# Keys and values from one pair of combined matrices in a fused two-layer block on one NeuronCore

## What is computed

```python
q = x @ Wq
k = x @ Wk
v = x @ Wv
latent_kv = (k + v) @ W_down_kv
k_rec = latent_kv @ W_up_k
v_rec = latent_kv @ W_up_v
...
qh, kh, vh = (heads(q), heads(k_rec), heads(v_rec))
...
scores = jnp.einsum('bhqd,bhkd->bhqk', qh, kh) * scale
...
decay = jnp.exp(-LAMBDA_DECAY * TIME_STEP * jnp.abs(idx[:, None] - idx[None, :]))
scores = scores * decay[None, None, :, :]
...
attn = jax.nn.softmax(scores, axis=-1)
```

## Time and profile before

| | |
|---|---|
| median of 3 runs | 816.33 us (816.19 to 817.85) |
| profiled execution, its own time | 818.78 us |
| its span, first to last instruction | 817.0 us |
| mean granted TensorE clock | 0.919 |
| TensorE busy | 703.0 us (86%) |
| ScalarE busy | 574.4 us (70%) |
| VectorE busy | 496.3 us (61%) |
| GpSimd busy | 261.1 us (32%) |

### The profile page before, as it was taken

One profiled execution on the slowest core, in us unless ns is written; L12 is line 12 of the kernel. 1 busy time (PEld: TensorE's weight loads), 2 busy tenths in 40 slices (PEclk: granted clock), 3 DMA queues, 4 the chain that ended last, 5 costly groups with the idle time before them and its releaser, 6 DMA issues.

```text
span 817.0 us, 11157 instructions
## 1 busy us (share of the span) xinstructions
PE 703.0 (86%) x3624; PEld 410.8 (50%) x3624; DVE 496.3 (61%) x1268; ACT 574.4 (70%) x807; POOL 261.1 (32%) x289
## 2 busy tenths in 40 slices
PE   2789889899898998999686697999999999999587
PEld 2566566576566676778454342223323232233364
DVE  4799879788787988889565542234323232222474
ACT  4657675656777666656444436999999999999243
POOL 3376466665666564556403000021200000000020
PEclk9999999999999999999657776999999999999958
DMA  9002322222233333333100269100079300000001
GB/s 260 3 0 67 91 91 91 78 93 76 80 95 88 91 104 103 95 116 104 51 1 0 58 138 195 23 1 1 1 144 193 79 1 1 1 1 1 3 1 51
DMA packets 31342, 54.53 MB, mean 67 GB/s; under 512 B 4625, under 2 KB 13281, under 8 KB 29777
## 3 DMA queue, kind: packets, MB, share of 16 engines
q1 hardware_dynamic: 30128, 53.38, 25.1%
q0 software_dynamic: 224, 0.34, 0.2%
q10 hardware_dynamic: 928, 0.06, 0.1%
HBM read 35.71 MB, written 1.28 MB: 45 GB/s over the span
## 4 chain that ended last, share of the span: by engine, by line
ACT 28%; PE 17%; issue 7%; DVE 6%; POOL 2%; ACTq 0%; POOLq 0%; DVEq 0%
ACT raw_w L827 25%; PE bank L1391 3%; PE bank L1392 2%; PE bank L1393 2%; PE bank L1680 1%; ACT xt L644 1%; POOL act_parts L574 1%; PE bank L1431 1%; PE bank L1515 1%; PE bank L1512 1%; PE bank L1587 1%; PE bank L1513 1%; PE bank L1446 1%; PE bank L1664 1%; DVE xn_parts L920 1%
## 5 line engine op out<-in xcount | busy, mean ns | idle before, releaser
L827 ACT ACTIVATE raw_w<-bank,minus_c 128x1024 f32<-128x1024 f32 x256 | 259.6, 1165 | 4.8 <-DVE bank L1271 2.6
L574 POOL TENSOR_TENSOR act_parts<-act,act_parts 128x512 fp32r<-128x512 f32 x128 | 167.7, 1312 | 147.4 <-ACT act_parts L716 142.0
L1271 DVE TENSOR_TENSOR bank<-bank,fix 128x256 f32<-128x256 f32 x128 | 55.3, 433 | 180.7 <-PE bank L1664 180.7
L702 ACT ACTIVATE bank<-bank,b_gate 128x512 f32<-128x512 f32 x112 | 74.1, 661 | 86.1 <-PE bank L1393 85.9
L1391 PE MATMUL bank<-xn_parts,w_hi 128*128 128x512 f32 x256 | 110.4, 431 | 20.9 <-DVE up L1044 11.5
L1393 PE MATMUL bank<-xn_parts,w_hi 128*128 128x512 f32 x256 | 104.3, 407 | 0.0
L1392 PE MATMUL bank<-xn_parts,w_lo 128*128 128x512 f32 x256 | 104.0, 406 | 0.0
L716 ACT ACTIVATE act_parts<-act 128x512 fp32r<-128x512 f32 x128 | 80.3, 628 | 23.4 <-DVE act L1062 21.9
L1044 DVE TENSOR_SCALAR up<-bank,b_up 128x512 f32<-128x512 f32 x113 | 84.0, 744 | 20.5 <-PE bank L1393 19.3
L1062 DVE SCALAR_TENSOR_TENSOR act<-up,bank 128x512 f32<-128x512 f32 x128 | 87.9, 687 | 4.4
L520 POOL TENSOR_SCALAR var_eps<-mean_var 128x4 f32<-128x4 f32 x28 | 7.2, 256 | 237.8 <-DVE mean_var L914 236.4
(11 more groups left out here) (198 smaller groups left out, 1089.2 us busy)
## 6 DMA issues: line engine op xcount, KB each, us to landing
grow<-scores SPq DMA_DIRECT2D x68, 256.0 KB, 3.2
early<-scores SPq DMA_DIRECT2D x44, 256.0 KB, 3.1
raw_w<-in_gate_up SPq DMA_DIRECT2D x4, 512.0 KB, 8.7
w_lo<-gelu_parts SPq DMA_DIRECT2D x8, 256.0 KB, 5.1
w_lo<-act_parts SPq DMA_DIRECT2D x8, 256.0 KB, 5.2
w_hi<-gelu_parts SPq DMA_DIRECT2D x6, 256.0 KB, 4.6
w_hi<-act_parts SPq DMA_DIRECT2D x6, 256.0 KB, 5.5
x_tok<-in_x SPq DMA_DIRECT2D x4, 256.0 KB, 4.4
```

Source lines behind the costliest of these rows:

```text
L574: pool.tensor_tensor(act_lo[:, j % NACT, :], act[:, j % NACT, :], act_hi[:, j % NACT, :].bitcast(F32), ALU.subtract).then_inc(s["lo_ready" ...
L702: eng.activation(out, bank[:, G, :], ACT.Gelu_apprx_sigmoid, bias=b_gate[:, e:e + 1]).then_inc(s["glu_ready"], 1)
L827: eng.activation(probs[:, u % NP, :], pair, ACT.Exp, bias=minus_c[:, b:b + 1])\
```

## The change

(Wk + Wv) W_down_kv W_up is worked out once, beside the expert loop. GpSimd adds Wk and Wv (slot 13). TensorE transposes the sum (slot 106), multiplies it with w_down (slot 109) and that with both w_up side by side (slot 112), in the bank `SIDE`; ScalarE copies each result out (slots 107, 110, 113) and the last one is split into `sq_hi` and `sq_lo`, the lo part by VectorE (slot 114), in place of Wk and Wv. Keys are then three passes from the norm, like queries, and values are three passes for each block of 128 tokens, straight from the norm. `keys_values` and `latents` and their copies are gone.

The low parts of queries and keys of chunks 0 and 1 move from VectorE to GpSimd. The copy of keys of chunks 2 and 3 moves from VectorE to ScalarE. Banks are given out anew (`Q_BANK`, `K_BANK`, `V_BANK`). The first products (`attn_first` on TensorE) are issued at step 12 of the skewed stage, in front of the transposes of chunk 3; the first operations of ScalarE and VectorE at step 13, in front of the hi and lo part of chunk 3. The table of powers has a semaphore of its own, `grow_loaded`.

The core of the diff, in the order of the file: tables and helpers, then the programs of GpSimd (`pool`), ScalarE (to `mix(step)` with `eng`), VectorE and TensorE (`pe`).

```diff
 SINGLE = {
-    "pe": {},
...
+    "pe": {"mix0": 106, "mix1": 109, "mix2": 112},
+    "act": {"split_small": -9, "split0": -6, "split1": -3, "split2": 0, "split3": 1, "split_squares": 11, "mix0": 107, "mix1": 110, "mix2": 113},
...
             for step in range(NC + max(stage.values())):
+                if step in once:
+                    once[step]()
...
+        Q_BANK, K_BANK, V_BANK = (4, 5, 0, 4), (6, 7, 1, 6), (3, 2, 3, 2)
...
                 pool.wait_ge(s["squares_hi_ready"], 1)
+                if half == 1:
+                    pool.tensor_tensor(w_kv[:], raw_s[:, WK, :], raw_s[:, WV, :], ALU.add).then_inc(s["w_kv_ready"], 1)
                 pool.tensor_tensor(sq_lo[:, at, :], raw_s[:, at, :], sq_hi[:, at, :].bitcast(F32), ALU.subtract)\
...
+
+            def query_lo(c):
+                if c == 0:
+                    pool.wait_ge(s["out1_ready"], NC)
+                for i in range(2):
+                    pool.wait_ge(s["q_hi_ready"], 2 * c + i + 1)
+                    pool.tensor_tensor(q_lo[:, i, place(c)], q_f[:, i, :], q_hi[:, i, place(c)].bitcast(F32),
+                                       ALU.subtract).then_inc(s["q_lo_ready"], 1)
+
+            def key_lo(c):
+                pool.wait_ge(s["v_ready"], c + 1)
+                for i in range(2):
+                    pool.wait_ge(s["k_hi_ready"], 2 * c + i + 1)
+                    pool.tensor_tensor(xn_parts[:, i, chunk(c)], k_f[:, i, :], k_hi[:, i, place(c)].bitcast(F32),
+                                       ALU.subtract).then_inc(s["k_lo_ready"], 1)
+
+            for c in range(QC):
+                query_lo(c)
+                key_lo(c)
             pool.wait_ge(s["bound_ready"], 1)
...
+            def key_raw(c):
+                eng.wait_ge(s["k_lo_ready"], 2 * QC)
+                eng.activation(raw_of(k_f, c), bank[:, K_BANK[c], :], ACT.Copy).then_inc(s["k_raw"], 1)
+
+            def attn_first():
+                query_squares(0)
+                query_hi(0)
 
             def attn_rest():
-                attn_first(0)
-                latents(0)
-                keys_values(1)
                 key_squares(0)
                 key_hi(0)
                 query_squares(1)
                 query_hi(1)
-                values_out(0)
-                latents(1)
-                keys_values(2)
                 key_squares(1)
                 key_hi(1)
+                values_out(0)
                 values_out(1)
                 query_squares(2)
-                latents(2)
-                keys_values(3)
                 key_squares(2)
+                key_raw(2)
+                query_squares(3)
+                key_squares(3)
+                key_raw(3)
                 values_out(2)
-                query_squares(3)
-                latents(3)
-                key_squares(3)
                 values_out(3)
...
+            def mix(step):
+                eng.wait_ge(s["mix_ready"], step + 1)
+                if step == 0:
+                    eng.activation(w_kv_t[:], bank[:, SIDE, 0:D], ACT.Copy).then_inc(s["mix_read"], 1)
+                elif step == 1:
+                    eng.activation(w_lat[:], bank[0:LAT, SIDE, 0:D], ACT.Copy).then_inc(s["mix_read"], 1)
+                else:
+                    eng.activation(sq_hi[:, WK:WV + 1, :].rearrange("p i d -> p (i d)"), bank[:, SIDE, 0:2 * D],
+                                   ACT.Copy).then_inc(s["mix_hi_ready"], 1)
...
-                    eng.wait_ge(s["prep_loaded"], 16 * (len(LATER) + 1))
+                    eng.wait_ge(s["grow_loaded"], 16)
+                else:
+                    eng.wait_ge(s["q_lo_ready"], 2 * c)
...
+            def key_decay(c):
+                eng.wait_ge(s["k_ready"], c + 1)
+                if c >= 1:
+                    eng.wait_ge(s["k_lo_ready"], 2 * c)
                 for i in range(2):
...
+                eng.wait_ge(s["q_lo_ready"], 2 * QC)
+                eng.tensor_copy(raw_of(q_f, c), bank[:, Q_BANK[c], :]).then_inc(s["q_raw"], 1)
+
+            def attn_first():
+                query_decay(0)
+                key_decay(0)
 
             def attn_rest():
-                query_decay(0)
-                query_lo(0)
-                key_decay(0)
-                key_lo(0)
                 query_decay(1)
-                query_lo(1)
+                key_decay(1)
                 maxima(0)
-                key_decay(1)
-                key_lo(1)
+                maxima(1)
                 query_raw(2)
-                maxima(1)
-                key_raw(2)
                 query_raw(3)
                 maxima(2)
-                key_raw(3)
                 maxima(3)
...
-            single = {"split_small": split_small, "powers": ssm_powers,
+            def mix():
+                eng.wait_ge(s["mix_hi_ready"], 1)
+                eng.wait_ge(s["squares_ready"], 2)
+                eng.tensor_tensor(sq_lo[:, WK:WV + 1, :].rearrange("p i d -> p (i d)"), bank[:, SIDE, 0:2 * D],
+                                  sq_hi[:, WK:WV + 1, :].bitcast(F32).rearrange("p i d -> p (i d)"), ALU.subtract)\
...
+            def ready(c):
                 pe.wait_ge(s["xn_ready"], nth_hi(LN_ATTN, c))
                 if c == 0:
                     pe.wait_ge(s["x_ready"], nth(X_FFN1A, NC - 1))
...
             def queries(c):
                 at = chunk(c)
-                if c >= 2:
-                    pe.wait_ge(s["maxes_ready"], c - 1)
-                split_matmul(bank[:, attn_banks(c)[0], :], sq_hi[:, WQ, :], sq_lo[:, WQ, :], xn_hi[:, at], xn_lo[:, at],
+                ready(c)
+                if c == 3:
+                    pe.wait_ge(s["maxes_ready"], 1)
+                split_matmul(bank[:, Q_BANK[c], :], sq_hi[:, WQ, :], sq_lo[:, WQ, :], xn_hi[:, at], xn_lo[:, at],
                              True, True).then_inc(s["q_ready"], 1)
 
-            def latents(c):
-                pe.wait_ge(s["prep_loaded"], 16 * (len(LATER) + 1))
-                pe.wait_ge(s["kv_copied"], c + 1)
-                pe.matmul(bank[0:LAT, attn_banks(c)[2], :], w_down[:], kv_f(c), start=True, stop=True)\
-                  .then_inc(s["lat_ready"], 1)
-
             def keys(c):
-                pe.wait_ge(s["lat_copied"], c + 1)
-                pe.matmul(bank[:, attn_banks(c)[3], :], w_up[:, 0, :], lat_f(c), start=True, stop=True)\
-                  .then_inc(s["k_ready"], 1)
+                at = chunk(c)
+                ready(c)
+                if c == 3:
+                    pe.wait_ge(s["maxes_ready"], 1)
+                split_matmul(bank[:, K_BANK[c], :], sq_hi[:, WK, :], sq_lo[:, WK, :], xn_hi[:, at], xn_lo[:, at],
+                             True, True).then_inc(s["k_ready"], 1)
 
             def values_in(c):
+                ready(c)
+                if c == 1:
+                    pe.wait_ge(s["xn_ready"], nth_hi(LN_ATTN, NC - 1))
+                elif c >= 2:
+                    pe.wait_ge(s["v_copied"], c - 1)
...
+                    at, out = slice(c * CH + 128 * t, c * CH + 128 * (t + 1)), bank[:, V_BANK[c], 128 * t:128 * (t + 1)]
+                    last = split_matmul(out, xn_hi[:, at], xn_lo[:, at], sq_hi[:, WV, :], sq_lo[:, WV, :], True, True)
                 last.then_inc(s["v_ready"], 1)
...
+                if c < QC:
+                    pe.wait_ge(s["q_decayed"], 2 * c + 2)
+                    pe.wait_ge(s["k_decayed"], 2 * c + 2)
                 else:
-                    pe.wait_ge(s["q_decayed"], 2 * c + 2)
-                pe.matmul(bank[:, attn_banks(c)[0], :], same_head[:], squares(c)[0], start=True, stop=True)
-                pe.matmul(bank[:, attn_banks(c)[2], :], same_head[:], squares(c)[1], start=True, stop=True)\
+                    pe.wait_ge(s["q_raw"], c - QC + 1)
+                    pe.wait_ge(s["k_raw"], c - QC + 1)
+                pe.matmul(bank[:, Q_BANK[c], :], same_head[:], squares(c)[0], start=True, stop=True)
...
+            def attn_first():
+                queries(0)
+                keys(0)
+                queries(1)
+                keys(1)
+                values_in(0)
+
             def attn_rest():
-                keys_values(0)
-                queries(0)
-                latents(0)
-                keys_values(1)
-                keys(0)
-                values_in(0)
-                queries(1)
-                latents(1)
+                pe.wait_ge(s["xn_ready"], nth_hi(LN_ATTN, NC - 1))
+                values_in(1)
                 norms(0)
-                keys_values(2)
-                keys(1)
-                values_in(1)
                 queries(2)
-                latents(2)
+                keys(2)
                 norms(1)
-                keys_values(3)
-                keys(2)
                 values_in(2)
                 queries(3)
-                latents(3)
+                keys(3)
                 norms(2)
-                keys(3)
                 values_in(3)
                 norms(3)
+
+            def mix(step):
+                if step == 0:
```

(15 more changed lines are left out.)

100 lines of the change are left out of this document (28 added, 72 removed), and 1 row of the table SINGLE.

## The result

| | before | changed |
|---|---|---|
| median | 817.09 us (4 runs, 816.19 to 818.02) | 802.26 us (4 runs, 800.54 to 805.89) |
| profiled execution | 818.78 us | 801.57 us |
| its span, mean granted clock | 817.0 us, 0.919 | 799.8 us, 0.931 |

The ratio is 0.983, 95% interval 0.980 to 0.986: faster, by 14.8 us in the medians and 17.2 in the profiled executions. I had said 801.2.

A forecast was written before the change was run, and what follows sets the result against it. It took a chain of waits as the bound, with 42.6 us from the last normalized chunk to the first exponential as its subject. 818.78 - 16.1 + 1.0 = 803.7, less 2.45 for the median: 801.2 us, range 797.5 to 806.5.

The forecast's parts named there:

- The removed and added products: TensorE per chunk: 8.3 us (low clock) or 4.4 (high) go; keys 1.3 or 0.7, values 2.6 or 1.3 come.
- the steps by hand: From chunk 2's transposes, followed in old trace times: fourth maximum starts at 472.75 instead of 488.85, gain 16.1 us.
- I take low from 466: TensorE's clock before the fourth maximum: high from 454, low again from 466 because of idling.
- the first rival: TensorE's clock stays high from 454 to the end of the section: 798.5 us; chance 20%.
- GpSimd: Low parts moved from VectorE, one pair of four on the path: worth 1.6 us at the fourth maximum.
- it becomes the bound: Rival: all eight of GpSimd's low parts on the path cost 5.0 us, so 806.2; chance 5%.
- +1.0: Expert loop: added TensorE products cost 0.86 us, with less well hidden weights 1.0; ends 0.5 and 1.5.
- Behind it: After the fourth maximum: stacks land before first scores at 478.5, and 20 us remain at VectorE's first wait for all four.
- The slower rival: Exponentials stay at the low clock, 0.31 us lost per piece; gain gone from 49 pieces (65 us); 100 pieces 832; 3%.
- The sum: Whole kernel: profiled 818.78 less 16.1 plus 1.0 is 803.7; 2.45 off for the median gives 801.2.

The follow-up runs named there:

- late mixing: Changed kernel with transpose and first product of the merged matrix moved to slots 122 and 128, second product into the next stage; median 800.74 us.
- no mixing: Changed kernel without making the merged matrix, keys and values from the plain matrices (other numbers); median 801.16 us.

## Why the prediction was right, point by point

The forecast of 801.2 held (802.26), and the range. The mechanism was right: the same links stand in the chain. The clock's value, GpSimd's and the loop's terms were off, and what I had not priced went the other way, so the closeness is partly luck; the last point has the sum.

- **The removed and added products, and the steps by hand.** Right in kind: first product 0.76 us behind chunk 2's transposes, small products 0.11 apart, the same links in the chain. (In the sum of what goes, the low clock gives 8.5 us per chunk by my own terms, not 8.3; the forecast doesn't use it.) Measured from the transposes, chunk 3's low part ended after 8.4 us, where the working had 9.2 (457.5 less 448.29) and the kernel before 5.7; the clock's rise, taken at 454, came within 452 to 454 (see the next point). That it ended 3.5 us later on the trace's clock is 2.7 of lateness and 0.8 of shift.
- **The clock**, "I take low from 466". In the profile of the result it stayed high; this was the first rival. The working gave 24.5 us to the maximum with the fall and 21.7 without. Measured were 20.63 without, and 24.05 and 24.36 where it fell at 463 to 465 (late mixing and no mixing, which share this stretch). There it rose again 1.7 and 1.8 us before the maximum, where I had let it stay low, and my steps were slow by themselves, so that 24.5 comes near is partly luck. That a fall costs some us was right; the step was wrong in treating as one value what differs between executions: four profiles of this stretch show 20.6, 22.7, 24.1 and 24.4. At the high clock my steps were also 1.1 us too slow, 0.8 of it because I let the clock rise 5.7 us behind the transposes and it rose after 4.1.
- **GpSimd.** Its key pair is on the chain once, as forecast, but worth 2.9 us instead of 1.6, compared at an equal clock. The difference is the four low parts of chunk 1 in front of the second maximum, as the rows above show; where my working put them, it doesn't say. That it becomes the bound did not come: it did its eight low parts from 454.1 to 465.7 and only VectorE's key decays of chunk 1 stood waiting for it before the maximum, 1.47 us.
- **The loop**, "+1.0". 1.5 us. The transpose took the 0.11 us worked out. Between GpSimd's same low parts in the two traces the first product (L1637, two records) moved the rest by 0.55 instead of 0.22, the second (L1639) by 0.83 instead of 0.53; each is 0.3 dearer. The trace shows the two records of each as one row, 0.41 and 0.69 us long; what makes them dearer wasn't tried.
- **Behind it.** Nothing waited for the stacks; 7.0 us from maximum to exponential; the clock stayed low over the first 7 us of the exponentials, then rose. The slower rival needed 65 us of it.
- **Not priced**: the stage behind the exponentials took 2.3 us more and the first stage behind the loop 0.8 less, both with the clock. With the loop's 1.6 and 0.4 less in the exponentials, the 19.9 us gained between chunk 2's transposes and the first exponential are 17.2 at the end.
- **The sum.** For the profiled execution I had 803.7, and it took 801.57. Up to the first exponential it gained 19.05 us where I had 15.1 (16.1 less 1.0), and lost 1.85 behind it where I had nothing. Then I took 2.45 off for the median, but this shift was no property of the kernel: the new median lies 0.69 above the profiled execution, and single executions of one kernel differ by 3 us and more. So 2.1 too slow and 3.1 too fast leave the 1.1 us by which the forecast missed.

## What to carry over

When a constant product of matrices stands inside a stage of round trips, working it out beside a loop can be worth far more than its own products: 1.5 us in the loop bought some 11 us net, since copies and waits went with it and the order could be drawn tighter. Where TensorE works in short pieces between waits, cost a step at both clocks and compare profiles only between marks at an equal clock; products that nobody reads, put into the waits, keep it high and here cost 0.2 us. Part a difference of totals by stages before you explain it: one unchanged stage differed here by 5 us from execution to execution. A helper engine twice as slow may still pay when it stands beside the chain: 2.9 us here, and up to 1.5 more once what it reads had a second buffer.

## What the runs showed that I had not expected

- The same kernel showed the clock high through the stretch in one profile and low from 455 to 462 in another, after nearly the same idle pieces.
- 5 to 14 unread products in the waits before the maximum went with a clock of 1.00 from its rise to the maximum in all five kernels that had them; of nine profiles without them, one stayed high.
- A saturated TensorE at the low clock delays the first exponentials by about 1.5 us in all: in the ten profiles that show it, the clock had risen again 6 to 9 us behind the first exponential.
- Loop ends of the same loop lay 5.5 us apart from profile to profile, while the last 53 us of it agreed within 0.1.
- The stage behind the exponentials, the same in all, took 50.4 us at a mean granted clock of 0.80, 53.8 to 53.9 at 0.71 and 55.2 to 55.7 at 0.65.
